# Counting equal edges earlier and in descending order, and moving 214 scatters of counts out of the attention sweeps

## The reference

```
x = layernorm(x + L0(x))   # attention over the edges of each node, once by receiver and once by sender
x = layernorm(x + L1(x))   # two typed attention layers (HGT): logits, segment softmax, weighted sum per receiver
x = layernorm(x + L2(x))   # GCN:  agg[d] = sum over edges of h[s] * dinv[s] * dinv[d]
x = layernorm(x + L3(x))   # GINE: agg[d] = mean over edges of (x[s] + edge term), then an MLP with batch norm
```

## Time and profile before

| | |
|---|---|
| median of the runs | 8375.03 us |
| the profiled execution | 8357.96 us |
| its span, first to last instruction | 8356.2 us |
| POOL busy, instructions | 5222.9 us (63%), 5419 |
| DVE busy, instructions | 5570.0 us (67%), 10955 |
| PE busy | 2793.5 us (33%) |
| ACT busy | 2920.7 us (35%) |
| stages by their first POOL instruction | `plc0` 1262, `l0` 2403, `t0` 3503, first sweep 3789, `t1` 5345, second sweep 5603, `t2` 7159, `dn` 7336 |

### The profile page before, as it was taken

How to read it: one execution, slowest core, us unless ns; L and a number is a source line. 1 busy time by engine, 2 the same in 40 slices (tenths; PEclk the granted TensorE clock), 3 DMA queues, 4 the chain that set the end, 5 groups by cost and what they waited for, 6 DMA issues and landing times. The chain is left out here.

```text
span 8356.2 us, 66957 instructions
## 1 busy us (share of the span) xinstructions
PE 2793.5 (33%) x19883; PEld 2195.0 (26%) x19883; DVE 5570.0 (67%) x10955; ACT 2920.7 (35%) x3159; POOL 5222.9 (63%) x5419
## 2 busy tenths in 40 slices
PE   5666644555510000090000000270000000479997
PEld 5666643555510000080000000270000000334443
DVE  7655536776669999887988877648777666702203
ACT  6333312333336666433333333233333333300101
POOL 2777777777777777556777777737777777500000
PEclk6555555555555555595555555585555555589998
DMA  4665404444446666555444444455444444356653
GB/s 118 224 206 182 165 21 131 132 132 136 133 130 222 218 213 221 181 192 176 145 144 144 144 144 144 128 190 168 140 145 140 144 144 139 95 139 190 196 186 109
DMA packets 482831, 1306.15 MB, mean 156 GB/s; under 512 B 156540, under 2 KB 251470, under 8 KB 428582
## 3 DMA queue, kind: packets, MB, share of 16 engines
q1 hardware_dynamic: 252742, 889.07, 31.2%
q0 software_dynamic: 199776, 358.27, 15.0%
q10 hardware_dynamic: 29952, 54.54, 2.6%
HBM read 782.92 MB, written 518.52 MB: 156 GB/s over the span
## 5 line engine op out<-in xcount | busy, mean ns | idle before, releaser
L1484 POOL DMA_INDIRECT l_swp_G<-table,KVI x1664 | 1579.0, 949 | 511.9 <-issue 506.3
L1741 PE MATMUL l_swp_AW<-l_swp_ET,ones 128*128 128x512 f32 x4 | 4.2, 1142 | 3093.2 <-DVE l_swp_ET L1719 3093.2
L1122 POOL DMA_INDIRECT arrived<-plc_QS,plc_idx x832 | 814.9, 979 | 253.6 <-issue 245.1
L1422 POOL DMA_INDIRECT adj<-VAL,CELL x832 | 809.9, 973 | 253.7 <-issue 253.1
L1122 POOL DMA_INDIRECT slots<-REC,plc_idx x832 | 796.8, 958 | 273.3 <-issue 251.9
L1207 POOL DMA_INDIRECT l_G<-table,OTHI x832 | 787.3, 946 | 256.1 <-issue 252.9
L961 PE MATMUL plc_pr<-plc_seen,plc_otf 128*128 128x49 f32 x3328 | 861.5, 414 | 12.4 <-DVE plc_seen L698 12.4
L961 PEld LDWEIGHTS plc_pr<-plc_seen,plc_otf 128*128 128x128 f32 x3328 | 846.7, 326 | 31.9 <-issue 31.7
L1741 PEld LDWEIGHTS l_swp_AW<-l_swp_ET,ones 128*128 128x128 f32 x4 | 1.0, 311 | 3093.6 <-DVE l_swp_ET L1719 3093.6
L1607 DVE TENSOR_TENSOR l_swp_PROD<-l_swp_G,l_swp_QS 128x1024 f32<-128x1024 f32 x208 | 253.4, 1218 | 594.2 <-DMA l_swp_G<-table,KVI 594.1
L1601 DVE SCALAR_TENSOR_TENSOR l_swp_QS<-l_swp_QS,KEEP,l_swp_QX 128x128 f32<-128x128 f32 x1664 | 589.8, 354 | 58.5 <-DVE CELL L1690 25.1
(11 more groups left out here) (518 smaller groups left out, 9280.7 us busy)
## 6 DMA issues: line engine op xcount, KB each, us to landing
sums<-l_ROW SPq DMA_DIRECT2D x104, 1088.0 KB, 5.1
l_swp_QX<-queries SPq DMA_DIRECT2D x104, 1088.0 KB, 8.1
dn_AR<-adj SPq DMA_DIRECT2D x100, 832.0 KB, 4.6
adj<-plc_zrow SPq DMA_DIRECT2D x100, 800.0 KB
dn_AR<-adj SPq DMA_DIRECT2D x100, 768.0 KB, 4.3
queries<-plc_zrow SPq DMA_DIRECT2D x55, 1088.0 KB
sums<-l_swp_ROW SPq DMA_DIRECT2D x52, 1096.0 KB, 5.2
plc_QX<-queries SPq DMA_DIRECT2D x104, 544.0 KB, 4.4
```

The source lines that it names most:

```text
L1122: pool.indirect_dma_start(out=slots, out_offset=bass.IndirectOffsetOnAxis(ap=idx[:, c % IB, j:j + 1], axis=0), in_=g.REC[:, c * CH + j, :] ...
L1422: pool.indirect_dma_start(out=g.cells, out_offset=bass.IndirectOffsetOnAxis(ap=g.CELL[:, g.put:g.put + 1], axis=0), in_=g.VAL[:, g.put:g.p ...
L1484: pool.indirect_dma_start(out=G[:, c % GR, j, :], out_offset=None, in_=table, in_offset=bass.IndirectOffsetOnAxis(ap=index[:, c * CK + j:c ...
```

## The change

- `later` and `cells` become functions of the module (`later`, `decide`) with their tiles in a class `Again`. The runs are taken in descending order of columns: run number k covers the columns from (103 - k) * 8 on. So the first runs have short comparisons in `later` and long searches in `max_index`, the last ones the reverse.
- The first READY = 16 runs are handled in `plc0`: from chunk 21 on, two columns in each of four chunks, and `decide` in the fifth, up to chunk 100. The first sweep handles runs 16 to 67, the second 68 to 103 in its first 36 steps and none in its last 16.
- POOL calls `put_cell` in a sweep 5 times a step and 6 times in every sixth step, from step 0 on: 269 calls instead of 376. The 16 and 8 calls at the merge stay. The other scatters are spread: 34 in `l0` (24 ahead of the merge, 5 between its two gathers, 5 behind), 52 in the last 27 tiles of `t0`, 88 in `t1` (one for each tile, two from tile 10 on), 72 in `t2`. Before it was 0, 0, 16 and 16.
- In `decide` the spare place is computed ahead of the chain instead of within it. `share` in `dn` reads the other column of `CNT`, which holds the same numbers as the graph is symmetric.

```diff
-BEHIND = 5
+READY = 16
+def run_at(k):
+    return (EC // 8 - 1 - k) * 8
+
+def later(v, g, b, k, i):
+    x = run_at(k) + i
+    if i >= 2:
+        v.wait_ge(b.told, b.n + i - 1)
+    if x == EC - 1:
+        v.memset(b.count[:, i:i + 1], 0.0).then_inc(b.told, 1)
+    else:
+        v.tensor_scalar(b.same[:, x % 2, 0:EC - 1 - x], g.KEY[:, x + 1:EC], g.KEY[:, x:x + 1], 0.0, ALU.is_equal, ALU.add,
+                        accum_out=b.count[:, i:i + 1]).then_inc(b.told, 1)
+
+def decide(v, g, b, k):
+    x = run_at(k)
+    at = slice(x, x + 8)
+    v.max_index(b.find[:, :], g.KEY[:, at], g.KEY[:, 0:x + 8]).then_inc(b.told, 1)
+    v.tensor_scalar(b.away[:, :], g.iota[:, 0:8], g.SPARE[:, 0:1], float(x), ALU.add, ALU.add).then_inc(b.told, 1)
+    v.wait_ge(b.told, b.n + 10)
+    v.tensor_scalar(g.VAL[:, at], b.count[:, :], 1.0, None, ALU.add).then_inc(b.told, 1)
+    v.scalar_tensor_tensor(out=b.drop[:, 0, :], in0=b.find[:, :], scalar=float(-x), in1=g.iota[:, 0:8],
+                           op0=ALU.add, op1=ALU.not_equal).then_inc(b.told, 1)
+    v.wait_ge(b.told, b.n + 12)
+    v.tensor_tensor(b.drop[:, 1, :], b.drop[:, 0, :], g.AGAIN[:, x // 8, :], ALU.max).then_inc(b.told, 1)
+    v.wait_ge(b.told, b.n + 13)
+    v.copy_predicated(g.CELL[:, at], b.drop[:, 1, :], b.away[:, :]).then_inc(b.told, 1)
+    v.wait_ge(b.told, b.n + 14)
+    v.sem_inc(g.celled, 1)
+    b.n += 14
...
@@ place_edges, DVE, chunk loop
+                    if 0 <= c - 21 < 5 * READY:
+                        if (c - 21) % 5 < 4:
+                            for i in (0, 1):
+                                later(v, g, again, (c - 21) // 5, (c - 21) % 5 * 2 + i)
+                        else:
+                            decide(v, g, again, (c - 21) // 5)
@@ layer0_sweeps, POOL, behind the gathers
+            for _ in range(24):
+                put_cell(pool, passed, g)
             for k in (0, 1):
+                if k == 1:
+                    for _ in range(5):
+                        put_cell(pool, passed, g)
                 pool.wait_ge(stored[k], 16 * NCK)
...
+            for _ in range(5):
+                put_cell(pool, passed, g)
@@ attention_sweep, POOL, in each step
-                if c >= BEHIND:
-                    for _ in range(8):
-                        put_cell(pool, passed, g, (part + 1) * NCK)
+                for _ in range(6 if c % 6 == 0 else 5):
+                    put_cell(pool, passed, g)
@@ attention_sweep, DVE
-                    if c >= 0 and x % 2 == 1:
-                        later(c, x // 2)
+                    if c >= 0 and x % 2 == 1 and first_run + c < EC // 8:
+                        later(v, g, again, first_run + c, x // 2)
...
-                if c >= 0:
-                    cells(c)
+                if c >= 0 and first_run + c < EC // 8:
+                    decide(v, g, again, first_run + c)
@@ turn_layer, POOL, t0 / t1 (t2: put_cell until all 832 are out)
                 for n in range(NB - AHEAD * GT + 1, NB):
                     put_query(n)
+                    put_cell(pool, passed, g)
+                    if n < NB - 2:
+                        put_cell(pool, passed, g)
...
                         put_query(n)
-                        put_cell(pool, passed, g, NCK)
+                        put_cell(pool, passed, g)
+                        if n >= 10:
+                            put_cell(pool, passed, g)
```

More of the change, by code:

```diff
@@ L464, in own_ends, with __init__, put_cell @@
     link(v.tensor_scalar(g.BACKI[:, k, :], small[:, 5:6], g.idle[:, 0:1], None, ALU.add))
+class Again:
+    def __init__(self, s, width):
+        self.told, self.n = s.sem("told"), 0
+        self.count = s.sb("again_count", [P, 8])
+        self.same = s.sb("again_same", [P, 2, width], BF16)
+        self.find = s.sb("again_find", [P, 8], U32)
+        self.drop = s.sb("again_drop", [P, 2, 8], U32)
+        self.away = s.sb("again_away", [P, 8], U32)
+def run_at(k):
[25 more added lines that the diff above has]
+    b.n += 14
+def put_cell(pool, passed, g):
+    if g.put < EC:
+        if g.put % 8 == 0:
+            pool.wait_ge(g.celled, g.put // 8 + 1)
+            passed()
+        x = run_at(g.put // 8) + g.put % 8
+        pool.indirect_dma_start(out=g.cells, out_offset=bass.IndirectOffsetOnAxis(ap=g.CELL[:, x:x + 1], axis=0),
+                                in_=g.VAL[:, x:x + 1], in_offset=None).then_inc(g.landed, 16)
+        g.put += 1
 def place_edges(nc, g, k, slots, tag, blank=(), empty=None, count=None, project=None, spread=None):
@@ L542, in place_edges @@
             field = s.sb("field", [P, EC], U32)
+            again = Again(s, P)
             odd = s.sb("odd", [P, 4])
@@ L1412, in _ @@
                 o.then_inc(added, 1)
[L1415 to L1424, removed]
 def attention_sweep(nc, g, k, table, width, index, voff, array, out, weights, tag):
-    part = 1 if weights else 0
+    first_run = READY + (NCK if weights else 0)
     ro = RO + 1 if weights else RO
@@ L1443, in attention_sweep @@
         weighed = s.sem("weighed")
[L1444 to L1449, removed]
+        again = Again(s, EC)
         init = s.sem("init")
@@ L1666, in carry @@
                 v.tensor_copy(X[:, 1 - c % 2, :, :, 0:1], X[:, c % 2, :, :, CK:CK + 1]).then_inc(carried, 1)
[L1668 to L1685, removed]
-                pick(v.scalar_tensor_tensor(out=DROP[:, 0, :], in0=FIND[:, :], scalar=float(-q * 8), in1=g.iota[:, 0:8],
-                                            op0=ALU.add, op1=ALU.not_equal))
-                v.tensor_tensor(DROP[:, 1, :], DROP[:, 0, :], g.AGAIN[:, q, :], ALU.max)
-                pick(v.tensor_scalar(AWAY[:, :], g.iota[:, 0:8], g.SPARE[:, 0:1], float(q * 8), ALU.add, ALU.add))
-                pick(v.copy_predicated(g.CELL[:, at], DROP[:, 1, :], AWAY[:, :]))
-                v.sem_inc(g.celled, 1)
             front = {0: last_maximum, 1: maximum, 2: shift, 3: fall, 4: cut}
@@ L1875, in _ @@
                     for _ in range(EC):
-                        put_cell(pool, passed, g, 2 * NCK)
+                        put_cell(pool, passed, g)
                     pool.wait_ge(lone, 16)
@@ L2564, in share @@
             def share():
[L2565 removed]
+                link(v.tensor_scalar(nodes[:, 2, :], g.CNT[:, 1, :], 1.0, None, ALU.max))
                 link(v.reciprocal(nodes[:, 2, :], nodes[:, 2, :]))
[L2567 removed]
+                v.tensor_tensor(nodes[:, 0, :], nodes[:, 2, :], g.CNT[:, 1, :], ALU.mult)
                 v.tensor_tensor(nodes[:, 1, :], nodes[:, 2, :], g.WSUM[:, :], ALU.mult).then_inc(lined, 1)
```

4 lines of the change are left out of this document (removed).

## The result

| | before | after |
|---|---|---|
| device time, median | 8374.16 us (8369.25 to 8377.86, 4 runs) | 8113.21 us (8109.71 to 8117.17, 4 runs) |
| profiled execution (span) | 8357.96 (8356.2) us | 8109.71 (8108.0) us |

The ratio is 0.9693, with a 95% interval of 0.9681 to 0.9705: 3.1% faster. The forecast was 8126 us, with a range of 8098 to 8178. Between the two profiled spans lie 248.2 us, where the sum said 248.9; between the medians lie 261 us.

What follows compares the result with a forecast made beforehand. POOL's back-to-back issue, 1.258 us an instruction, was taken to bound the sweeps. Terms: -264 + 1 + 0.5 + 3 + 2 + 8.6 = -248.9 us, from 8375.0 to 8126 us; range 8098 to 8178.

Steps and rivals of the forecast that it cites:

- POOL's count sets the sweeps: Both sweeps: POOL stays the bound; 107 scatters fewer per loop at 1.258 us, 269.3 us off, -264 us after a loss.
- The merge of the first sweep: End of first sweep: the merge's gather waits for the rows' store, so 5 us not gained, about 1 of it DVE's.
- DVE as the bound: Rival, 14%: DVE becomes the bound of the sweeps, 26.5 against 26.6 us a step; +20 to +55 us, about 8160.
- My sign of being wrong: POOL waits for DVE in a sweep (L1484 released by DVE), or t1 grows by over 10 us.
- The placing: Second placing: comparisons and searches added on DVE from chunk 21 to 100, covered by POOL's own pace; +1 us.
- Layer 0's merge, t0, t1: Scatters moved into POOL's idle time there: +0.5 us (0 to +6), +3 (0 to +8), +2 (0 to +21).
- the passages give back more: Rival, 13%: long instructions make t0 +8, t1 +21 and layer 0's merge +5: +29 us, 8154.
- t2: Last passage: 72 scatters at 1.53 us each outlast ACT; +8.6 us, between 0 and +8.6.
- All is paid in the passages: Rival, 2%: all 214 moved scatters cost 1.53 us each in the passages, 327 us against 264 saved: +63 us, 8438.
- The loop doesn't follow POOL: Rival, 3%: the wait on `celled` ahead of each sweep's loop, or something unseen, holds POOL; nothing gained: 8375.

Runs made afterwards that it cites:

- the ascending order: Changed kernel with columns counted in ascending order, so the longest comparisons come in the placing: 8106.30 us, against 8106.48 for the changed kernel.
- the order alone: Comparisons as in the changed kernel, POOL's scatters of counts where the kernel before had them: 8364.48 us, ratio 1.0004 to the kernel before.

## Why the prediction was right

The forecast and its mechanism held, and no rival took place: a run or a stage's own length speaks against each. That the sum met the spans within 1 us is luck. The sweeps gave 3.6 us less than forecast and the placing took 2 us more, the passages took 7 us less, and the two stages that the change doesn't touch differ by -1.3 and +3.3 us between the two profiles.

- *POOL's count sets the sweeps.* 104 scatters fewer between the first and the last gather, and 130.6 us less (1508.7 to 1378.1) in the first sweep: 1.256 us each, where 1.258 was used. The second sweep came out at -134.4 for -134.6.
- *The merge of the first sweep* was the one place where the size was off: I took 5 us as not gained, 8.6 were (134.6 - 126.0). The mis-sized part is DVE's: the merge's gather came 35.9 us after the last gather's end instead of 31.3, so 4.6 us later, where I had said 1. Without the comparisons it came after 28.3 us. The row of 9.35 us is that term, and filling it gave 9.3 us.
- *DVE as the bound* (14%): leaving out the comparisons changed the second sweep by 0.4 us. The estimate of 26.5 against 26.6 us a step was right for the dearest steps, and thin: in those steps DVE is no faster in the kernel without scatters in the loops, and the 46 us of room that it shows lie in the steps before. My sign of being wrong, gathers released by DVE, stands in the rows, but eight times 0.3 us is no wait.
- *The placing*: +3.1 us against +1. The eight profiles that have this placing on chips like the first have it at 1071.5 to 1075.4 us, 1074.0 on the mean, against 1072.3 in the one profile of before. So it costs some 2 us, if anything, and the cover was larger than needed, as the ascending order shows.
- *Layer 0's merge, t0, t1*: +0.6, -1.6 and +1.8 (+0.5, +3 and +2 predicted). My worry was stretched scatters in t0 and t1: a scatter there was busy for 1.058 and 1.050 us on the mean (over the timeline of POOL) against 0.968 in the sweeps, not the pace of t2. So *the passages give back more* (13%) didn't come. The reason that I gave for t1, little wide work of DVE, was wrong: 14 of its 88 scatters took over 1.1 us, and 10 of the 52 in t0. And the -1.6 us of t0 is no gain: without a scatter in it t0 took 284.1 us in the kernel with the order alone, and it lies between 284.0 and 287.9 in the profiles on these chips.
- *t2*: +6.3 of +8.6. I used 1.53 us an instruction; the 72 took 1.202 us on the mean and 0.30 between, 1.50 us. I had said that POOL would end last, and it does.
- *All is paid in the passages* (2%) would need the scatters in them on the path. Put there all at once, in t2, 158 of them cost 202.6 us; spread as in the change, 7 us.
- *The loop doesn't follow POOL* (3%): excluded by the first sweep's own length.

The absolute number missed by 13 us in the good direction (8113.21 for 8126). I put the difference on the median of before, 17 us above its profiled execution. After, the profiled execution lay only 3.5 us below the median. By medians the change gains 261 us, and 256 on the chip where both kernels were run again; by the one pair of profiled executions it gains 248. Which stage holds the 8 to 13 us between isn't shown, as before was profiled once; that one execution may simply have been a fast one.

On the stretched scatters, the timeline of DVE and POOL at two places of t2 in the changed kernel:

```profile
7055.77 1.08 DVE L2177 TENSOR_TENSOR t_OWN<-X,DINV 128x896 f32<-128x896 f32 x1
7055.96 1.72 POOL L526 DMA_INDIRECT adj<-VAL,CELL  x1 [0.30 <-issue]
...
7070.08 0.96 POOL L526 DMA_INDIRECT adj<-VAL,CELL  x1 [0.30 <-issue]
7070.16 1.09 DVE L2177 TENSOR_TENSOR t_OWN<-X,DINV 128x896 f32<-128x896 f32 x1
7071.35 0.95 POOL L526 DMA_INDIRECT adj<-VAL,CELL  x1 [0.30 <-issue]
...
7074.37 1.09 DVE L2180 TENSOR_TENSOR t_OWN<-t_OWN,HP 128x896 f32<-128x896 f32 x1 [1.01 <-ACT HP L2271]
```

The scatters of 7055.96 (1.72 us) and 7074.49 (1.80 us, shown above) start inside one of DVE's operations; those of 7070.08 and 7071.35 start just ahead of one and just after it, and take 0.96 and 0.95 us. The whole trace shows the same. 130 of POOL's indirect DMAs start inside one of DVE's operations on two tensors of 128x896, whose inputs both lie in SBUF. 96 of them take over 1.1 us, and each of these ends 0.81 to 0.87 us after DVE's operation. Of the other 34, eight start within 0.03 us of DVE's operation, and 26 when at most 0.26 us of it are left. Of the 31 that start inside a reduction of the same size, which has one input, none takes over 1.0 us. In the sweeps 203 of POOL's DMAs start inside the wide product L1666, and none takes over 1.1 us (0.953 us on the mean). That product has two inputs too, but the kernel keeps one of them, `QS`, in PSUM. The same holds for the 63 that start inside the products L2139 and L2154 of the passages, which read one input from PSUM. So in this trace what one of POOL's DMAs costs beside DVE goes with where DVE's inputs lie; no run moved an input to test it.

The Trainium skill ("SBUF — State Buffer", section "SBUF: two separate sides") has a DVE operation with two inputs in SBUF lock the shared ports against a GpSimd operation that reads SBUF, for the whole instruction. The trace agrees, if a scatter, which takes its indices and its counts from SBUF, counts as one that reads SBUF: it is held until DVE's operation is about to end. The same section infers that such an operation doesn't hold up the writing of descriptors; the busy time of the indirect DMAs here is held up all the same (1.72 against 0.96 us).

## What to carry to other kernels

When an engine issues back to back, its stage costs count times price; look then for stretches in which the same engine waits for others, and move the instructions that have no due time there, until the engine ends just after the one that it waited for. Leave the work in the loop only as far as its place there is free. Before you price such a move, find how late the operands are known: here DVE had to decide columns ahead of the first sweep, and that alone gained nothing, yet without it the 86 scatters of layer 0 and t0 could not have stood there. Check each filled gap on the timeline afterwards: one wait of 9.35 us was worth 9.3 us more. And look at the bound's nearest rival step by step, not over the whole stage: over the second sweep DVE seemed to have 170 us of room, and in its dearest steps it had about 0.2 us each.

## What the runs showed of the hardware that was not expected

- **The recorded clock of TensorE changed and no time did.** Slices of the page, before, after, and the changed kernel's other profile:

```profile
PEclk6555555555555555595555555585555555589998
```

```profile
PEclk9999999999999999998555555595555555599998
```

```profile
PEclk6555555555555555568555555595555555599998
```

In the second the record says full speed for the first half. From 1400 to 2400 us, in the placing, the granted clock is 0.50 before and 1.00 after (the lower and the upper level, 1.2 and 2.4 GHz), with the same work on TensorE. The means over the span are 0.582, 0.803 and 0.585. But the 3328 products of the placings, of 128x49, took 414 ns each in all three (861.5, 863.2 and 861.5 us together), and the four runs of the changed kernel at 0.803, 0.801, 0.585 and 0.586 took 8109.7, 8117.2, 8115.7 and 8110.7 us. For these small products the granted clock explains no time.

- **Chips differ more than the change.** 8362 us on two chips, 9740 us on a third, for the same kernel. POOL's instructions are not what differs (a scatter in the first sweep is busy for 0.967 us on the mean on both). What the third shows beside them are stops of DVE and ACT; that these are the whole difference isn't shown.
- **Comparisons don't slow POOL's issue.** With the longest of them running (6300 to 6400, DVE busy for 97.80 us), POOL issues 80 instructions in 100 us at 0.949 us each.
